# One gather in flight at a time in the last stage of a graph layer

## The reference, cut to what matters

```python
def reference(x, src, dst, edge_weight, shared_weight, output_bias):   # x: 100000 x 256, 25000 edges
    feats, cur = [x], x
    for _ in range(3):                                  # N_BLOCKS - 1
        msgs = edge_weight[:, None] * cur[src]
        cur = segment_sum(msgs, dst, num_segments=100000)
        feats.append(cur)
    y = concatenate(feats, axis=1) @ shared_weight + output_bias      # 1024 x 256 weights
    return layernorm(x + y)                             # over the 256 columns, no scale or shift
```

## Time and profile before

| what | value |
|---|---|
| median of three runs | 1546.35 us |
| profiled execution, span from first to last instruction | 1792.6 us; no other time of that execution is given |
| PE, DVE, ACT, POOL busy | 84%, 67%, 60%, 60% of the span |
| mean granted TensorE clock | 0.941 |
| DMA | 410.75 MB, mean 229 GB/s |
| last stage (D), by the gathers of tiles 24 to 188 | 1172.15 to 1727.62 us |

### The profile page before, as it was taken

One profiled execution on the slowest core, in us unless ns is written; L12 is line 12 of the kernel. 1 busy time (PEld: TensorE's weight loads), 2 busy tenths in 40 slices (PEclk: granted clock), 3 DMA queues, 4 the chain that ended last, 5 costly groups with the idle time before them and its releaser, 6 DMA issues. The chain is left out here.

```text
span 1792.6 us, 30951 instructions
## 1 busy us (share of the span) xinstructions
PE 1502.6 (84%) x7990; PEld 1239.2 (69%) x7990; DVE 1202.8 (67%) x4923; ACT 1083.3 (60%) x2674; POOL 1068.1 (60%) x1047
## 2 busy tenths in 40 slices
PE   7879888889888897679979998998878777778995
PEld 6767777777777775457757876876656666666784
DVE  6756566656565666777655665568879788877664
ACT  5656666656666662237755555656667666666675
POOL 4556656656666653745654777745656656656544
PEclk9999999999999997779999999999899899989997
DMA  7767777767777766348866877788887878877763
GB/s 261 224 213 222 232 219 235 225 213 239 222 231 232 223 215 189 86 151 282 268 221 188 239 218 209 192 245 280 281 271 268 269 254 274 285 254 255 238 223 120
DMA packets 214375, 410.75 MB, mean 229 GB/s; under 512 B 31044, under 2 KB 137533, under 8 KB 214202
## 3 DMA queue, kind: packets, MB, share of 16 engines
q1 hardware_dynamic: 164582, 311.03, 51.9%
q0 software_dynamic: 48624, 97.04, 19.7%
q10 hardware_dynamic: 996, 0.72, 0.2%
HBM read 227.02 MB, written 194.09 MB: 235 GB/s over the span
## 5 line engine op out<-in xcount | busy, mean ns | idle before, releaser
L1475 PE MATMUL ps_y<-w_sb,xT 128*128 128x256 f32 x2680 | 727.9, 401 | 70.1 <-DVE y_ring L1829 50.5
L1475 PEld LDWEIGHTS ps_y<-w_sb,xT 128*128 128x128 f32 x2680 | 500.2, 200 | 138.0 <-issue 54.3
L1829 DVE TENSOR_TENSOR y_ring<-ps_y,bias 128x512 f32<-128x512 f32 x391 | 269.0, 688 | 273.3 <-remote 137.2
L1185 ACT ACTIVATE o_ring<-y_ring,shift,rstd 128x256 f32<-128x256 f32 (+1 forms) x782 | 422.5, 590 | 0.0
L1835 DVE BATCH_NORM_STATS2 stats<-y_ring 128x6 f32<-128x256 f32 (+1 forms) x782 | 291.8, 416 | 4.2
L903 POOL DMA_INDIRECT tails_found<-tail_keys,table_idx x200 | 201.6, 1008 | 147.2 <-issue 60.9
L1172 ACT COPY xT<-ps_xT 128x512 f32<-128x512 f32 x279 | 160.3, 575 | 210.0 <-remote 128.5
L903 POOL DMA_INDIRECT rows_in<-in_x,gather_idx x200 | 200.6, 1003 | 128.7 <-issue 64.0
L903 POOL DMA_INDIRECT rows_in<-out_rows,early_node x160 | 164.6, 1029 | 156.2 <-DVE sums L2671 96.2
L907 POOL DMA_INDIRECT out_rows<-u_out,early_node x173 | 177.7, 1027 | 96.4 <-issue 50.0
L1464 PE MATMUL ps_xT<-ident,x_ring 128*128 128x128 f32 x1228 | 198.6, 287 | 27.1 <-ACT xT L1172 15.9
(11 more groups left out here) (352 smaller groups left out, 2301.0 us busy)
## 6 DMA issues: line engine op xcount, KB each, us to landing
x_ring<-in_x SPq DMA_DIRECT2D x195, 512.0 KB
out_rows<-o_ring SPq DMA_DIRECT2D x195, 512.0 KB
c_rows<-sums SPq DMA_DIRECT2D x49, 512.0 KB
u_rows<-u_out SPq DMA_DIRECT2D x49, 512.0 KB
keys_bc<-u_rows SPq DMA_DIRECT2D x21, 512.0 KB
listed<-u_rows SPq DMA_DIRECT2D x14, 512.0 KB
c_list_rows<-sums SPq DMA_DIRECT2D x11, 512.0 KB
u_out<-c_list_rows SPq DMA_DIRECT2D x44, 128.0 KB
```

What stands on the lines that cost most here:

```text
L1185: last = act.activation(o_ring[slot][0:rows, r * D:(r + 1) * D], y_ring[k][0:rows, r * D:(r + 1) * D], ACT.Identity, bias=shift[k][0:rows, ...
L1475: last = pe.matmul(ps_y[p % 2][0:rows, r * D:(r + 1) * D], columns_of(p)[0][:, q * P:q * P + rows], w_sb[:, c, :], start=c == 0, stop=c == ...
L1829: dve.tensor_tensor(y_ring[k][0:rows, half * 2 * D:(half + 1) * 2 * D], ps_y[half][0:rows, :], bias2[0:rows, :], ALU.add).then_inc(y_copie ...
```

## The change

In `gather_d`, every gather of the last stage after the one of tile 24 waits, beside what it waited for already, until the gather of the tile before it has landed in full.

```diff
--- before.py
+++ after.py
@@ -1090,6 +1090,9 @@
                     pool.wait_ge(ta_psum, n - Q + 1 - KEPT)
                 rows = UROWS * kept_window(n // Q)[1] if n < KEPT else N
                 limit(rows)
+                if n > EARLY:
+                    pool.wait_ge(tailx_in[(q - 1) % Q], 16 * ((n - 1) // Q) + 32)
+                    limit(rows)
                 index = (early_node if n < KEPT else tail_node)[:, n:n + 1]
                 gather(rows_in[q][:, :], out[0:rows, :] if n < KEPT else x[:, :], index, tailx_in[q])
```

## The result

The changed kernel takes 1871.44 us (median of four runs, 1867.7 to 1872.6) against 1548.4 for the kernel before: 1.208 times as long, 95% interval 1.206 to 1.210. The direction was forecast; the size, 323 us, lies outside the range of 1585 to 1830.

A forecast was written before the change was run, and what follows sets the result against it. VectorE and the transfers were taken as nearest to their limit. 163 x 4.3 + 3.5 = 704.4 us against 569.7 costs 134.7, on the median between 116 and 213; over 1546.35 this gave 1705 us, range 1585 to 1830.

The forecast's parts named there:

- The flight L: Last stage, gather's start to landing: half the gathers quiet (2.5 us), half caught by an SP burst (4.5), so 3.5.
- The reaction: GpSimd's delay from the end of a releasing wait to the next gather's start, 0.80 us, read from a restore.
- The room: Time from tile 25's gather to TensorE's turn of tile 188, 569.7 us profiled, 491.4 when scaled by 0.863.
- From the profile to the median: Cost on the timed runs: 116 us if everything shrinks alike, 213 if flights don't; a value between was taken.
- What bounds before: Last stage's long middle: no engine full, VectorE (241.7 of 300 us) and the transfers (81%) nearest to their limit.
- What is late next: Last stage: VectorE's restore waits for the landing, then bias, statistics, TensorE, ScalarE and SP; most of 135 us at L2671.
- They are late by the same amount: GpSimd's scatters behind a waiting gather are delayed equally; their tiles were normalised long before. No separate cost given.
- The scatter falls into the flight: On GpSimd, the scatter issued 1.33 us after its gather costs nothing, as long as its tile has been normalised.
- Hidden: Last stage: flights average 2.68 us or less, buffers still run ahead, no change, 1546 us; chance 9%.
- Every gather caught: Last stage: each landing's burst meets the next gather, flight 4.3 to 4.6 us, time 1776 or 1890; chance 14%.
- Faster: SP's loads and stores get the DMA engines more to themselves, 23.7 us of waits go, time 1526; chance 4%.
- The signs: Last stage: gathers 4 us or more apart, GpSimd idle about 320 us ahead of L903, DMA share about 65%.

The follow-up runs named there:

- e5_wait_behind: Changed kernel with the wait moved from ahead of the next gather to right behind its own gather, ahead of the scatter: 2007.89 us.
- e0_before: The kernel before, without any edit, profiled a second time: span 1549.2 us, run time 1551.1 us.
- e4_lag8: Changed kernel with each scatter issued four slots earlier, 8 tiles behind instead of 12: 1850.76 us.
- e8_three: Changed kernel with each gather waiting for the landing three tiles back instead of one: 1549.38 us, against 1549.62 for the kernel before beside it.

## Why the prediction was wrong, point by point

The mechanism was right in its core: gathers one at a time, at a pace of flight plus reaction. The cost was taken as 159 us and is 316 by the stage. The terms:

- *The flight L*, from the start of the gather's instruction to the landing, 3.5 from half quiet and half caught gathers: **the step that failed**. It was read from data packets, and GpSimd goes on only at the release. In e5_wait_behind, where 161 of 165 gathers have no other indirect transfer issued in their flight, the release comes 0.37 us after the last packet in the mean and 0.55 at most; in the changed kernel the median is 0.36, and for the gather at 1201.91 it is 0.5 (2.96 against 2.46). That time is neither in L nor in the reaction of the sum. To the release L is 3.93: the shorter half of the gathers has the mean 2.83 where 2.5 was taken, the longer half 5.02 where 4.5 was taken. 163 x 0.43 = 70 us.
- *The reaction*, 0.80 from a restore's end to the gather's start: 0.86 in the median and 0.91 in the mean, from the release. Nearly right; 163 x 0.11 = 18 us. With L it makes the pace, 3.93 + 0.91 = 4.84 where 4.3 was forecast.
- *The room*, 0.863 x 569.7 = 491.4: measured 476.4, so 15 us too little cost.
- *From the profile to the median*: the second step that failed. "A value between them" of 116 and 213 us was 159. The flight and the reaction of the changed kernel are no shorter than what was read from the first profile of before, so 213 was the right branch: 54 us lost by splitting. Together 159 + 70 + 18 + 15 + 54 = 316. Neither step alone carries the time past 1830: 1705 + 70 + 18 = 1793, and 1759 with the splitting mended.
- *What bounds before*: VectorE and the transfers were named as nearest; e0_before has VectorE at 93%, the DMA engines at 0.92, and TensorE at 91%. Right.
- *What is late next*: "the restore of the tile waits for the landing". Wrong in place: VectorE waited 3.0 us for landings and 199.3 for ScalarE. Nor was the lead all used up: the restores start a median of 7.2 us after the release of their rows (13.3 in e0_before). "They are late by the same amount" on the scatters missed that ScalarE waits for them to land. e4_lag8 shows that this wait costs at most 21 us; with it gone the restores do wait for the landings, and the pace stays GpSimd's.
- *The scatter falls into the flight*: right, e5_wait_behind.
- *Rivals.* Hidden: no; e8_three shows what it would take. Every gather caught gave 1776 to 1890 and so holds the measured time, but not for its reason: to the release the mean is 3.93 and not 4.3, and half of the gathers take 2.83. Faster: no sign of it.
- *The signs*: DMA share forecast about 0.65, is 0.57; GpSimd idle ahead of L903 forecast 320 us, is 357.0 for tiles to 159 and 64.8 for the rest; gathers forecast 4 us or more apart, are 4.84 in the mean, but quiet ones are 3.6 (1190.86 to 1194.45).

One row on the quiet side of L was misread. The late tile's 2.19 measured no full gather: from 1779.4 to 1779.8 us of the first profile of before GpSimd's queue moved 48 packets and hardly a byte, where the gather of the earlier trace rows has 0.11 MB in 48.

```profile
q0 software_dynamic: 48, 0.00, 7.8%
```

No gather of the changed kernel's stage had its release in less than 2.60 us.

## What to carry to other kernels

When a transfer's landing is put into a loop of one engine, the price per turn is flight plus the time from last packet to release plus the waiting engine's reaction; take all of it from a wait for a DMA of the same kind and size, start to start, and set it against the pace of the stage. Letting k flights overlap was free here once nearly all flights with their reaction, not only the mean one, fitted into k turns: three were enough and two were not. When a profile is scaled to a shorter median, do not shrink a latency with the rest unless a run shows that it shrinks. And check the profile's name for a releaser against the time of the release: in e4_lag8 it named VectorE for waits that the landing ended.

## What the runs showed of the hardware

- From the last packet of a gather to its release 0.37 us passed in the mean, 0.55 at most (161 gathers of e5_wait_behind with no other indirect transfer issued in their flight), and 0.84 to 1.05 us from the release to the start of the next gather's instruction (157 of 164 in the changed kernel, median 0.86).
- Flights were longer where the pace was faster, and overlapping them still paid: 5.74 us to the release with no limit (DMA share 0.92) and 3.93 with one in flight (0.57), at 2.80 and 4.84 us a tile. How much of this is overlap and how much SP's denser traffic is not separated; with lighter loads alone 3.93 became 3.49.
- TensorE's granted clock went with its idle time: from 1100 to 1450 us it was 1.00 in e0_before (busy 315.56 of 350 us) and 0.80 in the changed kernel (217.53 of 350). What the lower clock cost no run here separates; TensorE is not in the stretch of the chain shown.
